# Eight x loads of a post-layernorm block with a wait of their own each, and two unused SBUF tiles taken out

## The reference, cut to what matters

```python
q  = x @ Wq + bq                       # 1024 -> 1024, 16 heads of 64
kv = (x @ Wdown + bdown) @ Wup + bup   # 1024 -> 256 -> 2048, split in k and v
# rope turns q and k of a token by the same angle
att = softmax(einsum('bthd,btgd->bthg', q, k) / 8)
out = einsum('bthg,btgd->bthd', att, v) @ Wout + bout
x1  = layernorm(x + out)
h   = silu(x1 @ wg.T) * (x1 @ wu.T)    # 1024 -> 3072
y   = layernorm(x1 + h @ wd.T)
```

## Time and profile before

| | us |
|---|---|
| device time, median of 2 runs | 3732.49 (3713.78 and 3751.2) |
| device time of the profiled execution | 3713.67 |
| span of its slowest core (core 6), first to last instruction | 3712.1 |
| spans of its eight cores | 3680.4 to 3712.1 |
| PE busy, core 6 | 2743.5 (74% of the span) |
| DVE busy | 1721.4 (46%) |
| ACT busy | 771.2 (21%) |
| POOL busy | 292.2 (8%) |

### The profile page before, as it was taken

How to read it: one execution, slowest core, us unless ns; L and a number is a source line. 1 busy time by engine, 2 the same in 40 slices (tenths; PEclk the granted TensorE clock), 3 DMA queues, 4 the chain that set the end, 5 groups by cost and what they waited for, 6 DMA issues and landing times.

```text
span 3712.1 us, 41647 instructions; the slowest of 8 cores (3680.4 to 3712.1 us)
## 1 busy us (share of the span) xinstructions
PE 2743.5 (74%) x12447; PEld 1089.7 (29%) x12672; DVE 1721.4 (46%) x2582; ACT 771.2 (21%) x1331; POOL 292.2 (8%) x540
## 2 busy tenths in 40 slices
PE   0001787789877989688968987798769896899666
PEld 0000222223332333233323332333323332343222
DVE  2221455364554545463636454555545454636312
ACT  0000220313113221404041402331132204040201
POOL 0111000001000110011000100011001100110010
PEclk9999655779998999889988998899989998899778
DMA  7886000202331232213231224023322223132222
GB/s 198 242 242 175 18 1 23 66 23 63 91 85 52 65 90 77 71 47 90 69 99 35 66 89 113 24 64 91 80 63 60 84 77 82 49 84 73 91 80 85
DMA packets 108705, 303.97 MB, mean 82 GB/s; under 512 B 16192, under 2 KB 24768, under 8 KB 108496
## 3 DMA queue, kind: packets, MB, share of 16 engines
q1 hardware_dynamic: 61520, 169.14, 15.9%
q0 software_dynamic: 46976, 132.15, 12.7%
HBM read 269.77 MB, written 39.85 MB: 83 GB/s over the span
## 4 chain that ended last, share of the span: by engine, by line
PE 58%; DMA 13%; DVE 8%; issue 7%; ACT 4%; DVEq 0%; SPq 0%; another core or an unknown queue 0%; ACTq 0%; POOL 0%; POOLq 0%
PE P L708 9%; PE P L439 9%; PE P L724 9%; PE P L396 8%; PE P L386 8%; PE P L621 6%; DMA x_bf<-xt 3%; DMA wgb<-wg_s 3%; PE P L562 3%; DMA wub<-wu_s 3%; DVE esum L647 2%; DMA wqb<-wq_s 2%; PE P L762 2%; PE P L337 2%; DVE p_sb L673 2%
## 5 line engine op out<-in xcount | busy, mean ns | idle before, releaser
L673 DVE TENSOR_TENSOR p_sb<-P,vdup 128x512 bf16<-128x512 f32 x1024 | 693.7, 689 | 336.3 <-PE P L724 307.8
L386 PE MATMUL P<-x_bf,wgb 128*128 128x512 bf16 x1462 | 495.7, 410 | 102.1 <-DMA wub<-wu_s 82.5
L708 PE MATMUL P<-e_sb,selz_sb 16*128 16x512 bf16 x1024 | 439.1, 437 | 119.0 <-DVE e_sb L657 71.2
L724 PE MATMUL P<-p_sb,id_sb 128*128 128x256 bf16 x2048 | 493.5, 307 | 27.0 <-DVE p_sb L673 15.9
L396 PE MATMUL P<-x_bf,wub 128*128 128x512 bf16 x1463 | 497.0, 407 | 16.8 <-DVE h_sb L412 13.4
L596 DVE TENSOR_TENSOR hadb<-q_sb,krep 128x2048 bf16<-128x2048 bf16 x256 | 309.9, 1223 | 368.6 <-PE P L621 181.0
L439 PE MATMUL P<-h_sb,wdb 128*128 128x512 bf16 x1477 | 461.9, 383 | 15.9 <-DVE r_bf L448 12.6
L304 PE MATMUL P<-x_bf,wd_sb 128*128 128x512 bf16 x127 | 58.6, 564 | 428.0 <-DMA x_bf<-xt 427.7
L621 PE MATMUL P<-hadb,selred_sb 128*16 128x256 bf16 x2048 | 324.0, 277 | 46.9 <-ACT e_sb L608 21.0
L412 DVE TENSOR_TENSOR h_sb<-s_sil,P 128x512 bf16<-128x512 bf16 x192 | 131.1, 683 | 455.7 <-PE P L396 326.8
L405 ACT ACTIVATE s_sil<-P 128x512 bf16<-128x512 f32 x192 | 114.5, 596 | 929.7 <-PE P L386 875.6
(11 more groups left out here) (65 smaller groups left out, 1929.6 us busy)
## 6 DMA issues: line engine op xcount, KB each, us to landing
wdb<-wdn_s SPq DMA_DIRECT2D x64, 768.0 KB, 4.5
wgb<-wg_s POOLq DMA_DIRECT2D x192, 256.0 KB, 3.0
wub<-wu_s POOLq DMA_DIRECT2D x192, 256.0 KB, 3.0
wob<-wout_s SPq DMA_DIRECT2D x128, 256.0 KB, 3.0
wqb<-wq_s SPq DMA_DIRECT2D x64, 256.0 KB, 3.0
yt<-x2b SPq DMA_DIRECT2D x64, 256.0 KB, 3.2
stg<-wg SPq DMA_DIRECT2D x24, 512.0 KB, 5.0
stg<-wu SPq DMA_DIRECT2D x24, 512.0 KB, 5.2
```

The lines of the kernel that those rows point to most:

```text
L386: e.matmul(o, l, r, start=st, stop=sp)),
L673: add('V', (lambda e, o=o, a=a, b=b: e.tensor_mul(o, a, b)), waits=w, inc=s_v, d=640)
L708: e.matmul(o, l, r, start=True, stop=True)),
L724: e.matmul(o, id_sb[:, :], r, start=st, stop=sp)),
```

## The change

Three edits. The two unused tiles go, 2 KB of each partition, so that the tiles allocated after them have other addresses. Each x chunk c now waits for its own reader, `wo1[c]`, where before chunk 0 waited for the last of the eight and the others for nothing of DVE (`max(wo0[c], wo1[c])` is always `wo1[c]`, the later count). The wait of chunk 0 for the last L762 stays, as does the wait for the chunk two before.

```diff
-        erep = [E(nc.sbuf_tensor(f"erep{i}", [128, 512], BF16)) for i in range(2)]
...
                 if c == 0:
                     if ck['kv_pe_end']:
                         w.append((s_pe, ck['kv_pe_end']))
-                    if ck['wo_stt_end']:
-                        w.append((s_v, ck['wo_stt_end']))
+                if ck['wo_stt_end']:
+                    w.append((s_v, max(ck['wo0_list'][c], ck['wo1_list'][c])))
...
             ck['wo_stt_end'] = wo1[-1]
+            ck['wo0_list'] = wo0
+            ck['wo1_list'] = wo1
```

## The result

The changed kernel takes 0.9937 times the time of the one before, 95% interval 0.9918 to 0.9955: 23.4 us less on the 3713.67 of the profiled execution (16.7 to 30.5). The medians of all runs are 3699.6 us after and 3724.57 before. The forecast was 21.2 us less.

The account below looks back on a forecast made before the run. The chain was mostly PE work, with x loads 3% of the span, held at boundaries by DVE's late `wo1[7]`. Gaps of 25.40 us less 4.2 gave 21.2 off 3713.67, other terms 0: 3693 predicted, range 3669 to 3738.

Parts of the forecast that it names:

- Chunk 0's start: First x load at seven boundaries: goes out 0.6 us after the last L762, not after `wo1[7]`; 21.2 us earlier in all.
- 49 waits at nothing: New waits of chunks 1 to 7 at seven boundaries: already fulfilled, taken as 0 us, at most 10.3 us.
- It reaches the end of the chain: After the x loads: L304, L337, SP and DVE shift along with the earlier load, about 3.4 us at the third boundary.
- Near 84 less 20: Sign in the new profile: L304's idle for x, beside the start, near 84 us less 20.
- the forecast's own case: The main forecast without rivals: gain 21.2 us, bounds 0.5 to 31.6 us, so 3682 to 3713; chance 0.55.
- DVE's wait for the y store: DVE's x2b wait behind SP's queue at the third boundary: 10.94 us before, should read about 7.5.
- Other transfers: Earlier x loads meeting y stores on DMA: plus or minus 1.74 us at six boundaries, 10.4 us, taken as 0.
- the empty case: First boundary, with no y stores running: first x load took 3.16 us, set against 4.90 at the third.
- Tiles: Two unused tiles removed, later tiles move by 2 KB: at most 0.5 us either way, taken as 0.
- A: Rival at the boundaries: time not freed or taken back by a later wait; 3713 or 3710 us; chance 0.18.
- B: Rival on PE: shorter idle keeps the higher clock, L304 and L337 run faster; 3679 us; chance 0.12.
- C: Rival on the cores: granted clock falls over the stages; 0.011 eats all 21 us, 0.03 gives 3750; chance 0.15.

## Why the prediction was right, point by point

*Chunk 0's start.* Right, and so was its size. I took 0.6 us from the matmul to the load; the third boundary has 0.61, and read in the same way all seven boundaries of the slowest core have 0.61 or 0.62. The 21.2 us were added up on one core, the slowest; the eight cores have 19.0 to 21.7, and 20.4 in the mean. That the stall is DVE's order rather than L773's own work is shown by moving L773 alone (0.9957).

*49 waits at nothing.* Right for the time, as far as 0.38% can tell, and nearly right in fact: a fulfilled wait behind the awaited one costs 0.06 us, some 1.7 us in all, far from the 10.3 that were the upper bound. The forecast took 0 because three waits and one had the same gap in the earlier trace rows; but there the two fulfilled ones stand ahead of the awaited one in the program, and in the changed kernel they stand behind it.

*It reaches the end of the chain.* Right. Of the 20.4 us by which the loads start sooner, 19.1 arrive in the wait for x and in L304's own time, and the timed gain is 23.4 (16.7 to 30.5). "Near 84 less 20" is what the wait shows between the slowest cores of the two executions, 20.7 less, but on the mean of eight it lost 14.8, because L304's run got 4.3 us shorter, which the forecast's own case had left as it was. The nine L304 were to begin 3.4 us sooner after the last L762, and at the third boundary it is 4.1. The time moves with the start of the load in either direction (0.9789, 1.0143). One number was off: DVE's wait for the y store was to read about 7.5 us and reads 4.28. Of the 3.3 us between them, 1.7 come from SP's store, which goes out 12.3 us after the start of the nine L303 in place of 14.0; there the forecast's own case had left the sixteen L337 behind them at 5.70 us, and they took 3.61. The rest is the 4.1 us in place of 3.4, and that DVE got to its wait 0.9 us later, counted from the end of the last L761.

*Other transfers.* Plus or minus nothing was a fair value: from the first issue to the last landing the eight loads took 17.2 us in the mean of all boundaries and cores, and 17.1 before. One reading behind the bound was wrong. The 4.90 us of the earlier trace rows belong to the second load; the first one, issued at 1478.58, took 3.7, so that the 3.16 of the empty case was set beside the wrong load. After the change the first load took 3.07 us at this boundary.

*Tiles.* Right: 0.9991.

*Rivals.* A is excluded by the measured gain. B did not take place as it was told: the nine L303 still took 4.00 us at a granted clock of 0.50, while the chunks before them came in one by one. The sixteen L336 at the third boundary were faster than in the earlier trace rows, but over the program the time in which an L336 runs is 135.4 us on the mean of the cores, and was 134.7. What L303 gained, 4.3 us, goes with chunks that are there at its start, so that several run in a row (four at the third boundary). C did not take place: the cores' clocks lie at 0.895 to 0.903, against 0.890 to 0.900 before. With the Trainium skill's rule for the clock ("TensorE: Matmul & The Clock Gate", the section on the clock gate), that activity lifts it, the trace of the kernel with the own reader alone agrees: with the idle gone, the granted clock is 1.00 where L300 runs.

*What can be told.* The forecast held that a gain of 0.6% lies inside what a measurement of this kernel tells from no change. The interval is 0.37% wide in all, and it does tell them apart.

## What to carry to other kernels

A load into a buffer should wait for that buffer's last readers, chunk by chunk, and for nothing that only happens to be finished at the same time: the two waits that chunk 0 carried here, one for the last reader of all chunks and one for a matmul that reads no chunk, were worth 0.6% and a further 1.5%. When two independent streams of work share an in-order queue, look at what stands directly ahead of the instruction that releases a transfer: its own 0.5 us were no matter, the 3 us of another stream's wait ahead of it were. And look for such a wait in the rows around one boundary, since in the whole-program chain the line reads 3% before and after; but take its size from all boundaries and cores, since a single one is no guide (the 5.70 us of the sixteen L337 and the 5.0 us of the `wqb` load were both exceptions).

## What the runs showed that I had not expected

A late load costs more than its own wait. With the chunks landing singly, the matmuls L304 have a median of 586 ns, and the granted clock at the last of them is 0.50; with the chunks there beforehand the same 128 matmuls run at a median of 379 ns and a granted clock of 1.00. The time in which they run falls from 59.7 to 33.3 us, beside 65.8 us of wait.

A wait that is already fulfilled is nearly free, but not quite: 0.06 us each on a load's issue, the same at all boundaries and on all cores.

Half a microsecond of lead shielded a load of 256 KB from two of 768 KB at 40 of 48 places: from issue to landing it took 3.2 us (median) ahead of them and 6.9 behind them.
